# A conditional MLP on one core: two of four normalisations moved behind the next batch's first GELU, and two residual loads issued earlier

## The reference

```
NR  (0): out = gelu(x @ w1_nr  + b1_nr)  @ w2_nr  + b2_nr            512 hidden
TSR (1): out = gelu(x @ w1_tsr + b1_tsr) @ w2_tsr + b2_tsr           512 hidden
SR  (2): h   = gelu(x @ w1_sr  + b1_sr)                             1024 hidden
         out = gelu(h @ w2_sr + b2_sr) @ w3_sr + b3_sr
y   = x + out
res = (y - mean(y)) * rsqrt(var(y) + 1e-5) * gamma + beta
```

## Time and profile before

| | |
|---|---|
| median of 3 runs | 562.02 us (561.85 to 562.25) |
| profiled execution, time | 561.57 us |
| its span, first to last instruction | 559.8 us |
| TensorE busy | 549.4 us, 98% |
| VectorE, ScalarE, GpSimd busy | 267.7, 213.1, 254.6 us |
| DMA | 61.27 MB, mean 109 GB/s |

### The profile page before, as it was taken

One profiled execution on the slowest core, in us unless ns is written; L12 is line 12 of the kernel. 1 busy time (PEld: TensorE's weight loads), 2 busy tenths in 40 slices (PEclk: granted clock), 3 DMA queues, 4 the chain that ended last, 5 costly groups with the idle time before them and its releaser, 6 DMA issues. The chain is left out here.

```text
span 559.8 us, 8281 instructions
## 1 busy us (share of the span) xinstructions
PE 549.4 (98%) x2423; PEld 452.4 (81%) x2424; DVE 267.7 (48%) x417; ACT 213.1 (38%) x328; POOL 254.6 (45%) x225
## 2 busy tenths in 40 slices
PE   9999999999999999999999999999999999999994
PEld 6878887888888888888888888888888888888883
DVE  5661174865955856113610468212866105501656
ACT  5451335254253454214421452424255124513351
POOL 0879998575675576300430046700175300430056
PEclk9999999999999999999999999999999999999999
DMA  8875404444353443300330034400144200410032
GB/s 304 337 250 184 152 6 143 154 150 154 111 185 140 160 150 119 106 0 0 116 108 0 0 144 156 150 0 0 75 150 148 77 0 28 146 51 0 0 134 92
DMA packets 26225, 61.27 MB, mean 109 GB/s; under 512 B 3042, under 2 KB 3042, under 8 KB 26082
## 3 DMA queue, kind: packets, MB, share of 16 engines
q1 hardware_dynamic: 26208, 61.10, 31.2%
q10 hardware_dynamic: 2, 0.00, 0.0%
HBM read 44.31 MB, written 16.78 MB: 109 GB/s over the span
## 5 line engine op out<-in xcount | busy, mean ns | idle before, releaser
L456 DVE TENSOR_TENSOR g_lo<-bank,g_hi 128x512 fp32r<-128x512 f32 x112 | 77.4, 691 | 252.8 <-DVEq L117 252.8
L406 ACT ACTIVATE g_hi<-bank,bcol 128x512 fp32r<-128x512 f32 x112 | 77.8, 694 | 161.4 <-ACTq L117 160.2
L596 POOL TENSOR_TENSOR y<-y,row 128x512 f32<-128x512 f32 x64 | 95.2, 1507 | 51.0 <-POOLq L117 50.6
L600 POOL TENSOR_SCALAR var_eps<-mv 128x2 f32<-128x2 f32 x30 | 6.5, 218 | 227.6 <-POOLq L117 227.5
L428 ACT ACTIVATE y<-y,rstd 128x512 f32<-128x512 f32 x63 | 42.2, 717 | 172.0 <-ACTq L117 172.0
L236 PE MATMUL bank<-w_hi,g_hi 128*128 128x512 f32 x256 | 99.8, 390 | 1.2 <-PEq L117 1.2
L238 PE MATMUL bank<-w_hi,g_lo 128*128 128x512 f32 x256 | 99.7, 389 | 0.0
L237 PE MATMUL bank<-w_lo,g_hi 128*128 128x512 f32 x256 | 99.7, 389 | 0.0
L236 PE MATMUL bank<-x_hi,w_hi 128*128 128x512 f32 x240 | 93.5, 390 | 0.0
L237 PE MATMUL bank<-x_lo,w_hi 128*128 128x512 f32 x240 | 93.4, 389 | 0.0
L238 PE MATMUL bank<-x_hi,w_lo 128*128 128x512 f32 x240 | 93.4, 389 | 0.0
(11 more groups left out here) (42 smaller groups left out, 597.2 us busy)
## 6 DMA issues: line engine op xcount, KB each, us to landing
y<-x SPq DMA_DIRECT2D x64, 256.0 KB, 3.6
out<-y SPq DMA_DIRECT2D x64, 256.0 KB, 2.5
stage<-x_t SPq DMA_DIRECT2D x31, 512.0 KB, 3.3
w_raw<-weights SPq DMA_DIRECT2D x17, 512.0 KB, 4.7
row<-rows SPq DMA_DIRECT2D x1, 1280.0 KB, 11.4
stage<-x_t SPq DMA_DIRECT2D x2, 256.0 KB, 3.8
w_raw<-weights SPq DMA_DIRECT2D x2, 256.0 KB, 4.2
cond_sb<-cond ACTq DMA_DIRECT2D x1, 0.1 KB
```

The costliest lines, as they stand in the source:

```text
L406: eng.activation(g_hi[:, slot, :], psum, ACT.Gelu, bias=b)
L456: eng.tensor_tensor(g_lo[:, slot, :], psum, g_hi32[:, slot, :], ALU.subtract).then_inc(s_gs, 1)
L596: eng.tensor_tensor(y[:, t, :], y[:, t, :], row[:, kind, :], ALU.add).then_inc(s_xb, 1)
L600: eng.tensor_scalar(var_eps[:, t:t + n], mv[:, t:t + n, 1], EPS, None, ALU.add).then_inc(s_var, n)
```

## The change

ScalarE keeps a counter `turn` of the iterations in a register. In batch 0 it normalises all four tiles at the end as before. From batch 1 on it normalises tiles 0 and 1 at the end of the iteration, and leaves tiles 2 and 3 to the next iteration, where they come directly behind the first GELU pair (or, in kind NONE, which has none, at the start). In batch 1 nothing is left over from batch 0; batches 2 to 15 take over two tiles each. The last batch normalises tiles 0, 1 and 2 at its end, as before (tile 3 is finished by VectorE). Since ScalarE now releases a bank in every normalisation, also in kind NONE, TensorE takes the four releases in kind NONE. On SP, the loads of the first two residual tiles of batch 0 are issued directly behind the rows and ahead of the two x halves of batch 1; the other two stay behind them.

```diff
--- before.py
+++ after.py
@@ -195,11 +195,13 @@
                 load_pair(item)
             eng.dma_start(row[:, :, :].rearrange("p r h -> p (r h)"), rows.rearrange("r h -> (r h)").partition_broadcast(P)
                           ).then_inc(s_rows, 16)
+            load_row(0, 0)
+            load_row(0, 1)
             for f in range(2):
                 take(eng, s_stage[f])
                 load_x(x_halves[2 + f], f)
-            for t in range(TT):
-                load_row(0, t)
+            load_row(0, 2)
+            load_row(0, 3)
             landed = POOL_FIRST + POOL_ALL
             for item in POOL_ALL:
                 eng.wait_ge(s_loaded[landed[landed.index(item) - 2]], 16)
@@ -320,6 +322,7 @@
                 take(eng, s_x23, 2)
                 x_taken(1)
                 if kind == NONE:
+                    take(eng, s_acc, 4)
                     read_next()
                     return
                 if kind == TSR:
@@ -410,22 +413,51 @@
                 take(eng, s_full[f], 16)
                 eng.copy(x_hi[:, 2 * f:2 * f + 2, :], stage[:, f, :, :]).then_inc(s_hi, 1)
 
-            def body(kind, read_next, last):
+            def normalise(t):
+
+                take(eng, s_v)
+                eng.sem_inc(s_acc, 1)
+                take(eng, s_rstd)
+                eng.activation(y[:, t, :], y[:, t, :], ACT.Copy, scale=rstd[:, t:t + 1]).then_inc(s_n, 1)
+
+            def body(kind, read_next, b):
+
                 read_next()
                 for j in range(n_hidden(kind)):
                     gelu(bank[hidden_bank(kind, j)][:, :], j % 4, B1[kind] + j)
+                    if j == 0:
+                        normalise_late(b)
+                if kind == NONE:
+                    normalise_late(b)
                 if kind == SR:
                     for i in range(HC):
                         gelu(bank[i][:, :], i, B2[SR] + i, (1, 1, 2, 0)[i])
-                if not last:
+                if b is not END:
                     split_x(0)
                     split_x(1)
-                for t in range(FINISHED_BY_OTHERS_END if last else TT):
-                    take(eng, s_v)
-                    if kind != NONE:
-                        eng.sem_inc(s_acc, 1)
-                    take(eng, s_rstd)
-                    eng.activation(y[:, t, :], y[:, t, :], ACT.Copy, scale=rstd[:, t:t + 1]).then_inc(s_n, 1)
+                normalise(0)
+                normalise(1)
+                if b is END:
+                    normalise(2)
+                    return
+
+                with eng.If_cmp(turn, 0, "IS_EQ"):
+                    normalise(2)
+                    normalise(3)
+                eng.reg_add(turn, turn, 1)
+
+            END = NBATCH - 1
+            turn = eng.alloc_register("turn_Activation")
+            eng.reg_mov(turn, 0)
+
+            def normalise_late(b):
+                if b is END:
+                    normalise(2)
+                    normalise(3)
+                else:
+                    with eng.If_cmp(turn, 2, "IS_GE"):
+                        normalise(2)
+                        normalise(3)
 
             eng.dma_start(cond_sb[:, 0:NBATCH], cond.rearrange("(a b) -> a b", a=1)).then_inc(s_cond, 16)
             eng.wait_ge(s_power, 1)
@@ -446,8 +478,8 @@
             eng.wait_ge(s_const, 16)
             cond_of = first_condition(eng)
             with eng.Fori(0, NBATCH - 1) as b:
-                batch(eng, cond_of, b, lambda kind, read_next: body(kind, read_next, False))
-            batch(eng, cond_of, NBATCH - 1, lambda kind, read_next: body(kind, read_next, True))
+                batch(eng, cond_of, b, lambda kind, read_next: body(kind, read_next, b))
+            batch(eng, cond_of, END, lambda kind, read_next: body(kind, read_next, END))
 
         @block.vector
         def _(eng):
```

## The result

The changed kernel takes **571.42 us** (median of 6 runs, 570.65 to 572.75) against 562.03 us (561.69 to 562.25) for the kernel before in the same rounds: ratio 1.0168, 95% interval 1.0155 to 1.0181, slower by 9.4 us. The forecast was 567.3 with a range to 569.8: the sign was right, the size was about half of it, and the result lies above the range.

What follows compares the result with a forecast made beforehand. TensorE, busy 549.4 of 559.8 us, was taken to bound the kernel, so added waits are paid in full. Terms 4.5 + 0.35 + 0.4 = 5.25 us gave 567.3 us, range 564.3 to 569.8.

Steps and rivals of the forecast that it cites:

- part 1: Quiet NR batches: two normalisations behind the first GELU delay chunks 2 and 4, 0.90 us each, 4.5 us in all.
- parts 2 and 3: SR and TSR batches: the same move costs nothing; NR's later stores, reloads and bias additions: cost 0, covered by 2 us.
- Part 4: Batch 2: first GELU 0.74 us sooner, but chunks 2 and 4 wait; net +0.35 us, between -0.1 and +0.7.
- part 5: The counter and its compares elsewhere: register work of a tenth of a us, 0.05 hidden in batch 1; zero.
- part 6: Moved y loads delay batch 1's x halves; subtractions and additions take turns, residuals come later: +0.4 us (-0.6 to +1.7).
- the late-x rival: An instruction packet holds up an x half; batch 1 loses 1.7 us more instead of 0.4: 568.6 us; chance 0.12.
- the main case: All parts summed over the kernel, 5.25 us slower: 567.3 us, alone spanning 564.8 to 568.9; chance 0.75.
- the code rival: ScalarE's grown loop fetches code behind each NR batch's first GELU: 0 to 0.95 us each, at worst 572.1; chance 0.06.

Runs made afterwards that it cites:

- ScalarE's part alone: The changed kernel with the four residual loads back behind the second x, ScalarE as changed: 569.21 us, ratio 1.0124; run again 569.99 us, ratio 1.0146.
- the loads alone: The kernel before with only the two residual loads moved ahead of the second x: 562.18 us, ratio 1.0006.
- the four repeated runs: The changed kernel unaltered, measured once more on one chip: 570.73 us (568.67 to 572.68), ratio 1.0149.
- the padded kernels: The kernel before with 60 or 30 never-run instructions added to ScalarE's NONE body: 563.58 us (ratio 1.0034) and 563.44 us (ratio 1.0030).

## Why the prediction was wrong

**Right: the NR batches (part 1).** Forecast 0.90 each in batches 3 to 6 and 12, 4.5 in all; measured 0.97 and 4.83. The second GELU came 2.38 after the first (2.40 forecast), and the holes were where they were forecast. The normalisations' place was shown to be the cause by both kernels that moved them away.

**Right: parts 2 and 3.** SR and TSR batches behind batch 1 are unchanged, and so are the 7.7 us at the end. The late stores cost nothing with the leftover behind the first GELU; in batch 5 the first residual comes 18.6 us after the batch's start (19.5 forecast). The run with the leftover behind the fourth shows where that cover ends: in the last batch, 4.7 us.

**Part 4, batch 2: right by itself, wrong in place.** +0.35 was forecast, -0.61 came. Where batch 1 keeps its length (the other order of bodies, 54.40), batch 2 has its first GELU at +9.15 us (9.24 forecast) and loses 1.86 (1.9 forecast). In the changed kernel batch 1 ends 4.4 us later, GpSimd's chain of splits does not, and the hole that this change was to shrink closes without it. I summed the batches as if each kept its own; a delay in one was slack in the next, so that batch 2 came 0.96 us under its forecast.

**The step that failed: part 5.** "Register work of a tenth of a us", priced at zero, with 0.05 hidden. The instructions themselves are that cheap. But the grown code put the loop's end where code was not yet loaded: the jump took 3.16 us once, at the one place where the first GELU follows control directly. It cost 2.9 us more hole than before, and 1.67 in the profiled run since TensorE's clock fell behind a hole of 3.9 us: batch 1 lost 4.40 where 0 (part 5) and 0.4 (part 6) were forecast. I had the mechanism among the rivals, at 0.06, and put it at the wrong branch: behind the first GELU of every NR batch, where no wait ever came. What could have led to the right place is the earlier trace rows: the one stretch where ScalarE's control lay open on the path, with no other engine's work to cover it. The rule of the Trainium skill (Runtime: NRT & Kernel Launch, section Instruction fetch mechanics) that a taken branch to code outside the loaded pages waits for a fetch agrees with the traces: 2.5 to 3.2 us at the first jump to the loop's end, with two packets on the instruction queue in it (one in the first profile of ScalarE's part alone). That straight code waited too, 1.13 us, is what the kernel with the other order of bodies shows. The wait is paid once: later iterations jump over the same bodies, and in the changed kernel no later branch is followed by a gap of more than 0.7 us.

**Part 6, the loads: too small to be told from nothing.** Forecast +0.4 (bounds -0.6 and +1.7); measured alone +0.06%, an interval of -0.2 to +0.8 us, which holds the forecast and zero. The turns came as forecast: in the changed kernel add 22.29, subtract 23.01, add 23.55, subtract 24.59, then both residuals, at 26.82 and 27.42 (26.6 and 27.2 forecast). A subtraction took 2.31 us beside an addition and 1.21 alone. But the second residual comes 22.07 us after the batch's start with the loads alone, 21.35 and 21.17 in the two profiles of the changed kernel, 21.49 before: no fixed sign. The x halves were split at 21.8 and 23.1, later than the 20.8 and 22.1 expected. In the late-x rival x_lo was to be ready 0.6 us behind TensorE's need; it was ready at 26.9, 1.2 ahead of batch 1.

**The range.** Its upper end took the main case and a part of the code rival, not the two together with a fall of the clock. The six runs of the result all have a mean clock of 0.991 to 0.994. Two of the four repeated runs have 0.996, and these, 568.67 and 569.41, lie within the range; that would have been luck, since they too must have waited for code in batch 1 (argued: every profile of this code shows that wait).

## What to carry to other kernels

Work moved into an engine's idle time is free only on the side of the event that ends the idle time: here normalisations cost nothing ahead of the first GELU and 0.97 us a batch behind it, in the one kind whose chunks come in pairs. Code in a loop body has a price of its own where control first reaches a part that is not loaded; look for a place where the sequencer's path lies open between two engines, and let control get there while the engine is idle. Where TensorE waits for a normalisation that waits for GpSimd, mend GpSimd's order: for these conditions that gave 0.3%, the reordering on ScalarE lost 1.7%.

## What the hardware showed that was not expected

- Thirty never-executed instructions (loop end at instruction 201 instead of 171) brought a code wait of 2.5 us, sixty one of 2.75: it comes in a step. With the bodies in another order it came in straight code, at instruction 200.
- TensorE kept 2.4 GHz behind holes of 2.4 and 2.6 us (the padded kernels) and dropped to 1.2 GHz, with matmuls 0.427 us apart, behind each of the six of 3.8 to 4.2 us, for 3.4 or 6.8 us. The cost did not go with the hole's length: 2.6 us behind one of 3.78, 1.6 behind one of 4.17.
- With the same code ahead of it, TensorE's first x matmul came between 5.04 and 6.88 us in thirteen profiles. In twelve it follows directly behind small matmuls of a constant. The last fourteen of these took 0.98 to 1.10 us in eight profiles (first x matmul at 5.04 to 5.53) and 1.56 to 1.70 in four, the changed kernel's among them (5.98 to 6.07). TensorE's timeline before and changed:

```profile
4.50 0.99 PE L366 MATMUL bank<-const-bfloat16-1.0 128*128 128x128 bf16 x14
4.61 1.70 PE L369 MATMUL bank<-const-bfloat16-1.0 128*128 128x128 bf16 x14
```

Kernels with and without the changed ScalarE code are in both sets. In the thirteenth (6.88) the first x matmul waited 1.34 us for VectorE's split of a weight. What makes the fourteen slow in some executions stays open.
